# Head-mixed attention with a routed layer on Trainium2: scores in two 64-row blocks of the array, and the softmax bound written by VectorE

## What is computed

```python
qkv = x @ Wqkv.T + bqkv                              # q, k, v: (b, 16, n, 16)
q, k = apply_rope(q), apply_rope(k)
logits = einsum('bhid,bhjd->bhij', q, k) * SCALE
logits = einsum('bhij,gh->bgij', logits, Wpre)       # heads mixed before
attn = softmax(logits, axis=-1)
attn = einsum('bhij,gh->bgij', attn, Wpost)          # and after
out = einsum('bhij,bhjd->bhid', attn, v)
x = layernorm(x + out @ Wout.T + bout)
...
x = layernorm(x + ffn(x))                            # 16 experts, 16 slots each
```

## Time and profile before

| | |
|---|---|
| median of three executions | 8595.84 us |
| the profiled execution: its span | 8594.9 us |
| TensorE matmul busy | 8315.6 us, 97% |
| VectorE busy | 7684.5 us, 89% |
| ScalarE busy | 7251.8 us, 84% |
| GpSimd busy | 6719.8 us, 78% |
| mean granted TensorE clock | 0.984 |
| DMA, mean over the span | 16 GB/s |

### The profile page before, as it was taken

One profiled execution on the slowest core, in us unless ns is written; L12 is line 12 of the kernel. 1 busy time (PEld: TensorE's weight loads), 2 busy tenths in 40 slices (PEclk: granted clock), 3 DMA queues, 4 the chain that ended last, 5 costly groups with the idle time before them and its releaser, 6 DMA issues.

```text
span 8594.9 us, 399875 instructions
## 1 busy us (share of the span) xinstructions
PE 8315.6 (97%) x158060; PEld 4655.0 (54%) x158060; DVE 7684.5 (89%) x11341; ACT 7251.8 (84%) x13696; POOL 6719.8 (78%) x14053
## 2 busy tenths in 40 slices
PE   8999999998999999999899999999989999999997
PEld 4555555555455555555545555555554555555554
DVE  7999999997899999999789999999978999999996
ACT  6898989896689898989569899898957989898895
POOL 7788888884788888888478888888847888888883
PEclk9999999998999999999899999999989999999998
DMA  0000000002000000000200000000020000000002
GB/s 32 7 7 9 8 8 9 9 8 76 18 6 7 9 8 9 7 9 8 76 18 6 8 9 8 9 7 9 8 76 18 6 8 9 9 8 8 9 8 81
DMA packets 98674, 141.23 MB, mean 16 GB/s; under 512 B 7840, under 2 KB 88352, under 8 KB 94496
## 3 DMA queue, kind: packets, MB, share of 16 engines
q1 hardware_dynamic: 96800, 115.48, 4.0%
HBM read 73.51 MB, written 39.85 MB: 13 GB/s over the span
## 4 chain that ended last, share of the span: by engine, by line
PE 73%; DVE 10%; issue 9%; POOL 4%; ACT 2%; DVEq 0%; POOLq 0%; ACTq 0%
PE psS L1193 47%; PE psP L1213 15%; PE psO L1228 6%; DVE big L848 3%; DVE pl L876 3%; DVE top L839 2%; PE psM L1239 1%; ACT big L676 1%; DVE ot L859 1%; PE psS L1359 1%; PE psS L1330 1%; POOL pl L524 1%; PE psM L1254 1%; POOL at L452 0%; PE psS L1165 0%
## 5 line engine op out<-in xcount | busy, mean ns | idle before, releaser
L848 DVE SCALAR_TENSOR_TENSOR big<-psP,big 128x512 f16<-128x512 f32 x4096 | 2623.2, 682 | 303.7 <-ACT big L676 266.6
L676 ACT ACTIVATE big<-psP 128x512 f16<-128x512 f32 x4096 | 2199.0, 588 | 646.0 <-PE psP L1213 646.0
L839 DVE TENSOR_REDUCE top<-psS 128x1 f32<-128x1024 f32 x2048 | 2491.8, 1217 | 246.8 <-PE psS L1193 246.5
L1193 PE MATMUL psS<-KH,AH 128*128 128x512 f16 x8192 | 2465.7, 383 | 64.3 <-POOL AL L465 41.7
L1193 PE MATMUL psS<-KH,AL 128*128 128x512 f16 x8192 | 2441.9, 380 | 0.0
L1193 PE MATMUL psS<-KL,AH 128*128 128x512 f16 x8192 | 2441.0, 380 | 0.0
L657 ACT ACTIVATE pr<-psS,nb 128x1024 f32<-128x1024 f32 x2048 | 2283.9, 1115 | 67.8 <-POOL pl L524 1.4
L686 ACT ACTIVATE ph<-pr 128x1024 f16<-128x1024 f32 x2048 | 2165.3, 1057 | 64.7
L876 DVE TENSOR_TENSOR pl<-pr,ph 128x1024 f16<-128x1024 f32 (+1 forms) x2048 | 2149.0, 1049 | 1.3 <-issue 1.2
L1213 PEld LDWEIGHTS psP<-rh,ph 64*128 64x128 f16 x32768 | 1434.1, 95 | 857.2 <-DVE big L848 488.7
L1213 PE MATMUL psP<-rh,ph 64*128 64x64 f16 x32768 | 1681.9, 192 | 62.4 <-DVE big L848 54.0
(11 more groups left out here) (136 smaller groups left out, 7489.1 us busy)
## 6 DMA issues: line engine op xcount, KB each, us to landing
ph<-in_xT SPq DMA_DIRECT2D x16, 512.0 KB, 7.8
xr<-in_x SPq DMA_DIRECT2D x64, 128.0 KB, 2.1
Q<-in_w SPq DMA_DIRECT2D x8, 1024.0 KB, 7.3
out<-V SPq DMA_DIRECT2D x16, 512.0 KB, 3.8
d_x<-x SPq DMA_DIRECT2D x60, 128.0 KB, 2.0
d_xn<-xn SPq DMA_DIRECT2D x60, 128.0 KB, 2.3
d_lg<-lg SPq DMA_DIRECT2D x60, 128.0 KB, 2.0
d_ct<-cT SPq DMA_DIRECT2D x60, 128.0 KB, 1.7
```

The source lines that it names most:

```text
L676: a.activation(PT[:, hf * JH:(hf + 1) * JH, :, 0, i0:i0 + HQ], psP[:, ih, :].rearrange("p (j g i) -> p j g i", j=JH, g=H), ACT.Copy, scale ...
L839: v.tensor_reduce(top[:, t % 2, h:h + 1], psS[:, 2 * h:2 * h + 2, :].rearrange("p c n -> p (c n)"), X, ALU.max).then_inc(s_mx, 1)
L848: v.scalar_tensor_tensor(out=PT[:, js, :, 1, i0:i0 + HQ], in0=psP[:, ih, :].rearrange("p (j g i) -> p j g i", j=JH, g=H), scalar=MDROP, in ...
L1193: mm = pe.matmul(psS[:, c, :], A_[:, k8, k, :], K_[:, k, c * CW:(c + 1) * CW], start=n == 0, stop=n == 5)
```

## The change

Scores are contracted in blocks of 64 rows. The two blocks of the array (`tile_position` rows 0 and 64) work on different key positions: for half `hp` of the keys, block 0 fills bank 2hp and block 1 bank 2hp + 1, with 12 steps of a matmul in each, 24 a half instead of 12, of 512 columns as before. So every block needs all 256 channels of the queries in four steps (`KQ`). GpSimd writes the two it has on its own rows (`AX[:, t, 0:KT]`), and two DMAs a tile copy the other two from the other 64 rows. Keys are laid out to match: chunk 2hp's keys on one order of row halves and chunk 2hp + 1's on the other, which the start makes by multiplying in two 64-column blocks, each from its own chunk of x. That needs both chunks of a pair loaded, rotation tables by pair (`cosk`, `sink`, which lie in `AX`'s memory and are loaded after the last scores of a batch), and keys, queries and values in another order. GpSimd waits for the last rotated key before it writes the first queries.

VectorE's `half_max` is now one `tensor_tensor_reduce`: (score + lift) x (-SSCALE), with a running minimum as its result, straight into `nb`; the elementwise result goes to `spare` and isn't used. ScalarE's `bound` and the tensor `top` are gone. The output pieces are joined, 0 with 1 and 2 with 3, each after a half's scores.

```diff
+        axf = AX[:, :, :, :, :].rearrange("p t q s n -> p (t q s n)").bitcast(F32)
+        cosk, sink = (axf[:, i * NP * CW:(i + 1) * NP * CW].rearrange("p (c n) -> p c n", c=NP) for i in range(2))
...
             for b in range(B):
-                for c in range(2, NC):
-                    sp.wait_ge(s_v, b * (NC * 2) + 2 * (c - 1))
-                    keys_load(b, c)
+                sp.wait_ge(s_k, b * (2 * NC) + 4)
+                keys_load(b, 2)
+                sp.wait_ge(s_v, b * (2 * NC) + 4)
+                keys_load(b, 3)
...
+                def exchange(it, t):
+
+                    T = (b * NIT + it) * TI + t
+                    k8 = t % TG
+                    sp.wait_ge(s_A, T * 4 + 4 + 1)
+                    for half in range(2):
+                        mine, other = slice(half * HP, (half + 1) * HP), slice((1 - half) * HP, (2 - half) * HP)
+                        sp.dma_start(AX[mine, k8, KT:KQ, :, :], AX[other, k8, 0:KT, :, :]).then_inc(s_ax[k8], 16)
...
+                for t in range(LEAD):
+                    exchange(0, t)
+                for it in range(NIT):
+                    for t in range(TI):
+                        if it < NIT - 1 or t + LEAD < TI:
+                            exchange(it + (t + LEAD) // TI, (t + LEAD) % TI)
+                        if t == 3 and it >= 1:
+                            row_load(it)
+                        for r, at in in_work(it):
+                            if t - 1 == at.get("norm"):
+                                store_normed(r)
+                            if t - 1 == at.get("turn_c"):
+                                store_routed(r)
...
-                    g.tensor_copy(AH[:, t % TG, :, :], at[:, :, :]).then_inc(s_A, 1)
+                    g.tensor_copy(AX[:, t % TG, 0:KT, 0, :], at[:, :, :]).then_inc(s_A, 1)
...
-                    g.tensor_tensor(AL[:, t % TG, :, :], at[:, :, :], AH[:, t % TG, :, :],
+                    g.tensor_tensor(AX[:, t % TG, 0:KT, 1, :], at[:, :, :], AX[:, t % TG, 0:KT, 0, :],
                                     ALU.subtract).then_inc(s_A, 1)
...
-                def bound(T, t, h):
-
-                    p = t % 2
-                    a.wait_ge(s_mx, T * 2 + h + 1 + 1)
-                    a.activation(nb[:, p, h:h + 1], top[:, p, h:h + 1], ACT.Copy, bias=LIFT * math.log(2.0),
-                                 scale=-SSCALE).then_inc(s_nb, 1)
...
-                    v.wait_ge(s_S, T * NC + 2 * h + 2)
-                    v.tensor_reduce(top[:, t % 2, h:h + 1], psS[:, 2 * h:2 * h + 2, :].rearrange("p c n -> p (c n)"),
-                                    X, ALU.max).then_inc(s_mx, 1)
+                    v.wait_ge(s_S, T * 2 + h + 1)
+                    v.wait_ge(s_nb, T * 2 + h + 1)
+                    apart(v)
+                    v.tensor_tensor_reduce(out=spare[:, :], in0=psS[:, 2 * h:2 * h + 2, :].rearrange("p c n -> p (c n)"),
+                                           in1=lift[:, 0:1].broadcast_to([P, N2]), scale=-SSCALE, scalar=-LOW,
+                                           op0=ALU.add, op1=ALU.min,
+                                           accum_out=nb[:, t % 2, h:h + 1]).then_inc(s_nb, 1)
...
+                                mm = pe.matmul(psS[half * HP:(half + 1) * HP, 2 + f, :], wqk_s[:, k, w0:w0 + HP],
+                                               xT_s[half][:, k, :], start=k == 0, stop=k == KT - 1,
+                                               tile_position=(0, half * HP))
...
+                for c in range(NC):
+                    for work in ((queries, values, keys), (keys, queries, values))[c % 2]:
+                        work(c)
...
+                    if hp == 0:
+                        pe.wait_ge(s_ax[k8], ((b * NIT + it) * 2 + t // TG) * 32 + 32)
                     if not fresh:
-                        pe.wait_ge(s_exp, (T - 1) * 2 + c // 2 + 1 + 1)
-                    n = 0
-                    for A_, K_ in ((AH, KH), (AL, KH), (AH, KL)):
-                        for k in range(KT):
-                            mm = pe.matmul(psS[:, c, :], A_[:, k8, k, :], K_[:, k, c * CW:(c + 1) * CW],
-                                           start=n == 0, stop=n == 5)
-                            n += 1
+                        pe.wait_ge(s_exp, (T - 1) * 2 + hp + 1 + 1)
+                    steps = [(s_, K_, kq) for s_, K_ in ((0, KH), (1, KH), (0, KL)) for kq in range(KQ)]
+                    for n, (s_, K_, kq) in enumerate(steps):
+                        for half in range(2):
+                            rows = slice(half * HP, (half + 1) * HP)
+                            mm = pe.matmul(psS[:, 2 * hp + half, :], AX[rows, k8, kq, s_, :], K_[rows, kq, hp, :],
+                                           start=n == 0, stop=n == len(steps) - 1, tile_position=(half * HP, 0))
                     mm.then_inc(s_S, 1)
...
-                        scores(T, t, 0, first and t < 1)
-                    pieces(0)
-                    if live:
-                        scores(T, t, 1, first and t < 1)
-                    pieces(1)
+                        scores(T, it, t, 0, first and t < 1)
+                    pieces(0, 1)
```

More of the change, by code:

```diff
@@ L237, in seq_layer @@
         s_A = sem("s_A")
+        s_ax = [sem(f"s_ax{k}") for k in range(TG)]
         s_S = sem("s_S")
-        s_mx = sem("s_mx")
         s_exp = sem("s_exp")
@@ L337, in tables @@
                 sp.dma_start(sin_s, sin_t).then_inc(s_w, 16)
+                for half in range(2):
+                    rows = slice(half * HP, (half + 1) * HP)
+                    for dst, src in ((cosk, cos_t), (sink, sin_t)):
+                        by_pair = src[rows, :].rearrange("p (c two n) -> p c two n", c=NP, two=2)
+                        sp.dma_start(dst[rows, :, :], by_pair[:, :, half, :]).then_inc(s_w, 16)
             def keys_load(b, c):
@@ new lines, in _, with rope @@
+                    b0, b1_ = bqk_s[:, 2 + 2 * part:3 + 2 * part], bqk_s[:, 3 + 2 * part:4 + 2 * part]
+                    def rope():
+                        for f, (q0, q1), bias in ((0, (kc0, ks0), b0), (1, (ks1, kc1), b1_)):
+                            v.wait_ge(s_k, b * (2 * NC) + 2 * c + f + 1)
+                            for dst, tab in (((q0, cosk), (q1, sink)), ((q0, sink), (q1, cosk)))[f]:
+                                v.scalar_tensor_tensor(out=dst, in0=psS[:, 2 + f, :], scalar=bias, in1=tab[:, pair, :],
+                                                       op0=ALU.add, op1=ALU.mult).then_inc(s_kp, 1)
+                        v.wait_ge(s_kp, base + 4)
+                        v.tensor_tensor(kr0, kc0, ks1, ALU.subtract).then_inc(s_rk, 1)
+                        v.tensor_tensor(kr1, ks0, kc1, ALU.add).then_inc(s_rk, 1)
@@ new lines, in v_bias @@
+                    def v_bias():
+                        for h in range(2):
+                            n_v = b * (2 * NC) + 2 * c + h
+                            v.wait_ge(s_v, n_v + 1)
+                            if c >= 1:
+                                v.wait_ge(s_vl, n_v - 1)
+                            v.tensor_tensor(vb[h].rearrange("p j g d -> p j (g d)"),
+                                            psP[:, h, :].rearrange("p (j d) -> p j d", j=2),
+                                            bv_s[:, :].unsqueeze(1).broadcast_to([P, 2, DIM]),
+                                            ALU.add).then_inc(s_vc, 1)
@@ L826, in _ @@
+                    for work in ((v_bias, rope), (rope, v_bias))[part]:
+                        work()
                     for k, kr in enumerate((kr0, kr1)):
                         v.wait_ge(s_kh, b * (2 * NC) + 2 * c + k + 1)
-                        v.scalar_tensor_tensor(out=KL[:, k, n_], in0=kr, scalar=KSCALE, in1=KH[:, k, n_],
+                        v.scalar_tensor_tensor(out=KL[:, part * KT + k, pair, :], in0=kr, scalar=KSCALE,
+                                               in1=KH[:, part * KT + k, pair, :],
@@ L1153, in _, with keys, queries @@
             with pe.Fori(0, B) as b:
-                pe.wait_ge(s_w, b * 64 + 64)
-                for c in range(NC):
+                pe.wait_ge(s_w, b * NW_DMA + NW_DMA)
+                def keys(c):
+                    part = c % 2
+                    for half in range(2):
+                        pe.wait_ge(s_xT[half], b * (8 * NC) + 16 * (c // 2) + 16)
+                    for f in range(2):
+                        if c >= 1:
+                            pe.wait_ge(s_kp, b * (4 * NC) + 4 * (c - 1) + 2 * f + 2)
+                        for k in range(KT):
+                            for half in range(2):
+                                w0 = (2 + f) * P + (half ^ part) * HP
+                                mm = pe.matmul(psS[half * HP:(half + 1) * HP, 2 + f, :], wqk_s[:, k, w0:w0 + HP],
+                                               xT_s[half][:, k, :], start=k == 0, stop=k == KT - 1,
+                                               tile_position=(0, half * HP))
```

(16 more changed lines are left out.)

76 lines of the change are left out of this document (34 added, 42 removed).

## The result

The changed kernel takes **8535.88 us** (median of four executions, 8529.52 to 8543.35) against 8596.99 (8595.69 to 8601.34): a ratio of 0.9928 with an interval of 0.9917 to 0.994. It is 0.7% faster, 61 us. The forecast was 8337, 259 us down, with a range from 8200 to 8500. The direction held, the size did not, and the time lies above the range. The profiled execution has a span of 8541.5 us, 53.4 less than that of before.

The account below looks back on a forecast made before the run. TensorE was taken to bound the kernel, VectorE close behind. From 8594.9 us, 277 (4.3 a pass, 64 passes) came off and 18 for batch starts went on: 8336, 8337 as median; range 8200 to 8500.

Parts of the forecast that it names:

- Rival E: Scores on TensorE: weight loads cannot run under matmuls of their own block, 2.36 us more a tile, 10,630 us; chance 0.04.
- A passage costs 0.105 us: TensorE switching between full array and 64-row blocks costs 0.105 us; 60 fewer a pass, a ceiling of 403 us.
- +0.02 us a call: VectorE's new pass with running minimum was to take 0.02 us longer to the next start than the reduction it replaces.
- Rival D: VectorE's new pass costs much more than the reduction, +0.5 us a call, making the kernel slower at 9095 us; chance 0.07.
- VectorE becomes the pace: Plain slots (one tile's work, no output product): VectorE needs 6.83 us, so they fall by 0.17, not 0.42.
- The exchange, hidden in the loop: The two query DMAs a tile, issued seven tiles (49 us) before use, cost nothing in the loop; 1.7 us a tile otherwise.
- Output slot: 10 before, 4 after, since pieces 0,1 and 2,3 are joined: Slots 2 and 10, with an output product: passages between array layouts fall from 10 to 4, saving 0.63 us each.
- Slot 4, "-0.21": The slot with the projection loses two of its four passages between array layouts and was to shorten by 0.21 us.
- TensorE can run ahead by some 0.4 us ... 0.8: Behind each of two output slots VectorE has caught up, so TensorE gains some 0.4 us before waiting, 0.8 a pass.
- Slots 14 and 15, -0.17 each: Two of the eight plain slots, each forecast to fall by 0.17 us, to 6.83.
- Rival C: GpSimd and VectorE hold each other up, plain slots stay at 7.0 us and other slots' passages count: 8479 us; chance 0.13.
- Start of a batch, 18 us: Per batch, 2.2 us waiting for exchanged queries and 2.3 us of exposed loads, 4.5 in all, 18 us for four.

## Why the prediction was wrong

- **"Twelve steps of two blocks ... are 12 x 0.216 = 2.59 us a half"**: right, 2.59. Rival E and the literal rule of the Trainium skill (TensorE: Matmul & The Clock Gate, Part 3) are out here too: 0.216 a pair with a load for each matmul of the same row block.
- **"A passage costs 0.105 us"**: right; TensorE's slots are 6.58 where nobody holds it.
- **"+0.02 us a call"**: slightly high, 1.21 + 0.08 us with no lengthening of VectorE's loop. Rival D is out.
- **"VectorE becomes the pace" at 6.83**: right in slots 0, 1, 8 and 9, at 6.74 to 6.78 us. Over a pass its share is 93% (114.51 of 122.70 us), not the 97% that I gave as a sign.
- **The exchange, hidden in the loop**: right; leaving it out shortens no slot.
- **"Output slot: 10 before, 4 after, since pieces 0,1 and 2,3 are joined"**, -0.63 each: **the step that failed.** I counted the passages that joining saves and took a run of 128 + 48 short matmuls at the rate of its parts. It isn't: code comes too slowly for it. In place of -0.63 each stand +0.33 and +0.16 by the means: (0.96 + 0.79) x 64 = 112 us of the 206 that the span is short of its forecast. The pauses themselves are some 82 to 97 of these (the run with the pieces apart, and the sum of the long pauses). The remaining 15 to 30 I can't split with certainty: VectorE, starved in the pause, has to catch up, and before the change it was busy 10.45 of the 11.35 us of slot 2.
- **Slot 4, "-0.21"**: wrong by the same kind of oversight, a saving of TensorE's booked where VectorE had no room. It went up by 0.49 (mean), since VectorE fills it: 0.70 x 64 = 45 us.
- **"TensorE can run ahead by some 0.4 us ... 0.8"**: a lead shows only in slots 3 and 7, which fell by 0.32 and 0.39 (means), 0.71 together, where their plain gain and the whole lead had promised 1.14: 27 us. What lead there was, slot 4 gave back.
- **Slots 14 and 15, -0.17 each**: nothing came, 22 us. Rival C's mechanism was named but taken for all plain slots or none; it holds where GpSimd has root steps. On the other side slots 0, 1, 8, 9, 12 and 13 gave some 22 us more than forecast.
- **Start of a batch, 18 us**: 34, and 3 more at the end of the program. The exchange's wait was right at 2.1 us a start, forecast 2.2, but without the exchange the starts are 4 to 5 us shorter each; how the rest divides between it and the loads stays open.

The range failed for one reason: it was built from prices of engines' work, and the unknown that decided, the joined pieces, was a change of order that I costed as pure gain with no bound on the other side. Its nearest row was at hand: before, no more than 112 short matmuls stood in a row.

That the pause is a lack of code rests on three things: it always ends 1.20 to 1.61 us behind a packet, it stands only at one place in 256 instructions, and three arrangements order it (176 short matmuls in a row: 91 long pauses in the tile loop; 128: 22; 112: 4, and none before the change). No run changed the loading of code itself. What stays open is what lies between a packet's end and the resumption, and how far ahead of its use code is fetched.

## What to carry to other kernels

When a change joins or reorders work on an engine, reckon the instructions per microsecond as well as the time of each: a run of short matmuls with a load for each can use up code faster than it arrives (here 129 instructions a microsecond against some 78), and shows up as "issue" within a run that has no wait. Before adding up what the first engine saves, write down for every slot what the second and third engines need there; a saving is cashed only in slots where all have room, and a lead gained in one is given back in the next full one. Two parts of a change may be worth 0.1% and nothing alone and 0.7% together, so undo them one at a time and do them one at a time.

## What the runs showed of the hardware

- TensorE pauses of up to 1.7 us appear within runs of matmuls 0.015 us apart, each with its load, mostly after 114 to 175 of them. All 91 long ones in the tile loop end 1.20 to 1.61 us after a 16 KB packet of code is through, and within a batch lie whole multiples of 256 instructions apart.
- Packets of TensorE's code start no less than 3.30 us apart in this trace, one pair of 1464 aside.
- Pairs of 512-column matmuls in two 64-row blocks, and of 512-column float32 matmuls in two 64-column blocks, run side by side at full rate.
- A pass over 1024 PSUM values with an elementwise result and a running minimum takes 1.21 us on VectorE, as long as a plain reduction over them.
